# Two message-passing layers on one core: the first edge stage moved to an edge-major tile, half- and quarter-array matrix products, and longer scans in the second edge stage

## The reference

```python
xs = jnp.concatenate([x[edge_src, :8], x[edge_dst, :8]], axis=1)
xv = jnp.concatenate([x[edge_src, 8:].reshape(E, 8, 3), x[edge_dst, 8:].reshape(E, 8, 3)], axis=1)
y1, y2 = _sph(edge_vec)
h = 2.0 ** 0.5 * jax.nn.relu(emb @ W1 / 10.0 ** 0.5)
w = (h @ W2 / 16.0 ** 0.5).reshape(E, 7, MUL, MOUT)
...
s_out = PW_S * (jnp.einsum('eu,euw->ew', xs, wa_s) + INV_SQRT3 * jnp.einsum('eui,ei,euw->ew', xv, y1, wb_s))
...
edge_ftr = jnp.concatenate([s_act, (gates[:, :, None] * v_out).reshape(E, 24)], axis=1) * norm[:, None]
return jax.ops.segment_sum(edge_ftr, edge_dst, num_segments=N)
...
e = s_src[src] + s_dst[dst]
e = jnp.where(e >= 0, e, LEAKY_SLOPE * e)
m = jax.ops.segment_max(e, dst, num_segments=N)
ex = jnp.exp(e - m[dst])
denom = jax.ops.segment_sum(ex, dst, num_segments=N)
alpha = ex / denom[dst]
out = jax.ops.segment_sum(h[src] * alpha[:, None], dst, num_segments=N)
```

## Time and profile before

| | us |
|---|---|
| median of three runs | 6804.19 |
| the profiled execution | 6803.31 |
| its span, first to last instruction | 6801.6 |
| stretch of the 400 groups of the first edge stage (545 to 4075) | 3530 |
| node stage (4090 to 4378) | 288 |
| gathers of the second edge stage (4378 to 6618) | 2240 |
| from its last gather to the next block (6618 to 6647) | 29 |
| last node stage (6647 to 6802) | 155 |

### The profile page before, as it was taken

One profiled execution on the slowest core, in us unless ns is written; L12 is line 12 of the kernel. 1 busy time (PEld: TensorE's weight loads), 2 busy tenths in 40 slices (PEclk: granted clock), 3 DMA queues, 4 the chain that ended last, 5 costly groups with the idle time before them and its releaser, 6 DMA issues. The chain is left out here.

```text
span 6801.6 us, 56405 instructions
## 1 busy us (share of the span) xinstructions
PE 3324.4 (49%) x12859; PEld 1615.4 (24%) x12859; DVE 3604.2 (53%) x5475; ACT 2499.0 (37%) x3555; POOL 4713.2 (69%) x4419
## 2 busy tenths in 40 slices
PE   0008999999999999999999980000000000000000
PEld 0004444444444444444444440000000000000000
DVE  5326887888888888888887872022222221222122
ACT  0006767666666666676766650000000000000000
POOL 4467777777777777777777727776666676677665
PEclk9999999999999999999999995555555555555555
DMA  3511111111111111111111100011111111111111
GB/s 144 179 37 27 31 30 31 29 31 31 27 31 30 31 31 27 29 31 30 31 31 29 22 13 18 10 21 27 27 25 21 29 26 25 24 27 26 25 24 24
DMA packets 266126, 228.09 MB, mean 34 GB/s; under 512 B 181312, under 2 KB 242565, under 8 KB 263406
## 3 DMA queue, kind: packets, MB, share of 16 engines
q0 software_dynamic: 121824, 79.09, 8.1%
q1 hardware_dynamic: 144082, 147.06, 6.7%
HBM read 137.59 MB, written 88.34 MB: 33 GB/s over the span
## 5 line engine op out<-in xcount | busy, mean ns | idle before, releaser
L1159 POOL DMA_INDIRECT gxb<-tab_d,idxb x1600 | 1536.2, 960 | 707.1 <-issue 652.5
L541 POOL DMA_INDIRECT gx<-in_x,idx x1540 | 1670.4, 1085 | 411.3 <-issue 370.9
L868 DVE TENSOR_TENSOR prod<-G_ps,hid 128x1000 f32<-128x1000 f32 x1200 | 1423.1, 1194 | 636.3 <-PE G_ps L744 297.2
L758 PE MATMUL R_ps<-sums,red 128*48 128x500 f32 x2400 | 1290.6, 621 | 0.0
L1251 PE MATMUL R_ps<-dm,ones 125*125 125x125 f32 x2 | 0.8, 494 | 2557.0 <-DVE dm L1280 2557.0
L637 ACT ACTIVATE FT<-T_ps 128x500 fp32r<-128x500 f32 x1200 | 706.9, 589 | 514.1 <-PE T_ps L727 309.1
L727 PE MATMUL T_ps<-ident,HL 125*128 125x125 f32 x4800 | 750.2, 279 | 251.8 <-ACT HL L631 171.8
L548 POOL TENSOR_TENSOR sums<-prod 128x500 f32<-128x500 f32 x400 | 503.0, 1257 | 505.5 <-DVE prod L868 304.0
L1166 ACT ACTIVATE ex<-ex 125x80 f32<-125x80 f32 x40 | 10.8, 269 | 2212.3 <-DVE one_d L1200 1433.6
L1212 DVE TENSOR_TENSOR_SCAN Zb<-dec,Zb,wx 125x40 f32<-125x40 f32 x1280 | 333.6, 294 | 721.1 <-issue 719.7
L727 PEld LDWEIGHTS T_ps<-ident,HL 125*128 125x128 f32 x4800 | 572.3, 143 | 466.1 <-ACT HL L631 172.1
(11 more groups left out here) (195 smaller groups left out, 4152.0 us busy)
## 6 DMA issues: line engine op xcount, KB each, us to landing
y_d<-Zb SPq DMA_DIRECT2D x40, 664.1 KB
gx<-in_x,idx POOLq DMA_INDIRECT x1600
gxb<-tab_d,idxb POOLq DMA_INDIRECT x1600
xd_d<-zeros SPq DMA_DIRECT2D x16, 1562.5 KB
xv<-xd_d SPq DMA_DIRECT2D x40, 625.0 KB
y_d<-zr SPq DMA_DIRECT2D x40, 625.0 KB
em<-in_edge_attr SPq DMA_DIRECT2D x40, 195.3 KB
kp<-keep_d SPq DMA_DIRECT2D x40, 156.2 KB
```

Of the source, the lines that this page charges most:

```text
L541: nc.gpsimd.indirect_dma_start(out=gx[h][:, c * DIM:(c + 1) * DIM], out_offset=None, in_=x, in_offset=bass.IndirectOffsetOnAxis(idx[h][:, ...
L758: last = Tn.matmul(R_ps[0:NOUT, 0:GW], red[:, i * NOUT:(i + 1) * NOUT], sums2[k][:, i * GW:(i + 1) * GW], start=(i == 0), stop=(i == 2))
L868: V.tensor_tensor(prod[i][:, :].rearrange("p (a e) -> p a e", a=2), gv, hid[k][:, :].rearrange("p (a e) -> p a e", a=2), ALU.mult).then_in ...
L1159: nc.gpsimd.indirect_dma_start(out=gx[h][:, c * T1:(c + 1) * T1], out_offset=None, in_=tab_d, in_offset=bass.IndirectOffsetOnAxis(idx[h][: ...
```

## The change

**First edge stage.** F and gx go. One tile `edge` holds 80 columns (a ring of 10 pieces of 8 columns) edge-major, 96 numbers of one edge side by side: 48 of the source end and 48 of the destination end. POOL gathers straight into it, from a copy of x with reordered features that the first block now writes to DRAM (xp_d). POOL does nothing else in the stage; a gather of a piece waits until `low` has read what lay in it. ACT places the scanned destination rows and the edge numbers. `turned` (two DVE products of 192 elements) and `along` (one DVE reduction of 384) take the place of the chunk-wide product and POOL's additions. `high` is two ACT copies of 384 for a piece, `low` two DVE subtractions of 384, and `low_again` goes.

PE transposes two tiles for a group instead of three, into two PSUM buffers, from overlapping 128-column windows of HL. The hidden part is one accumulated pair of matmuls on rows 64 to 127, and one relu; hid is 500 columns and is read twice by `multiply`. Each of the three products is four matmuls that use half of the array's rows: (l, a) = (0,0), (0,1), (1,0), (1,1), where a picks rows 0 to 63 or 64 to 127 and its own PSUM bank, and l the high or low part. The additions on DVE and POOL go. `reduce` is six float32 matmuls, each of which uses 32 of the 128 columns of the array, at i = 0, 1, 2 in turn. `back` reads 96 rows instead of 48. POOL's last step of the message (L561) goes to DVE.

**Second edge stage.** wx and Z are feature-major with a carry column ahead of each feature; three scans of 451 elements replace the 33 of 40. ACT copies the result into a tile of its own, zr, which SP stores.

```diff
-    NT = 3
-    QF = 80
-    FD = QF + NEMB
-    FW = NT * KF
-    HJ = HID // 2
+    SD = 48
+    EW = 2 * SD
+    NT = 2
     SB = 400
     ZEARLY = 12
-    EARLY = 60
+    EARLY = 7
...
+    sp.wait_ge(S("a_xp"), 2)
+    sp.dma_start(xp_d.rearrange("(p k) f -> p (k f)", k=NP), xp[0:P, :]).then_inc(S("a_tab"), 16)
...
+    V.tensor_copy(xpv[:, :, 8:32].rearrange("p k (a u) -> p k a u", a=3), xnv[:, :, 8:32].rearrange("p k (u a) -> p k a u", a=3)).then_inc(S("a_xp"), 1)
+    V.tensor_copy(xpv[:, :, 0:8], xnv[:, :, 0:8]).then_inc(S("a_xp"), 1)
...
+    def gather(s, t):
+        if s % PC == 0:
+            pool.wait_ge(S(f"b_idx{s // PC}"), t * 16 + 16)
+            pool.sem_inc(S("go"), 1)
+        for c in range(s * PW, (s + 1) * PW):
+            nc.gpsimd.indirect_dma_start(out=edge_c[:, c, 8:8 + DIM], out_offset=None, in_=xp_d,
+                                         in_offset=bass.IndirectOffsetOnAxis(idx[c // C][:, c % C:c % C + 1], 0)).then_inc(S(f"b_gx{s}"), 16)
+
+    for s in range(EARLY, RING):
+        gather(s, 0)
+    with pool.Fori(0, PAIRS - 1) as t:
+        for s in range(RING):
+            pool.wait_ge(S("b_lo"), t * RING + s + 1)
+            pool.sem_inc(S("go"), 1)
+            gather(s, t + 1)
...
+    def high(p, s, ch):
+        act.wait_ge(S("b_al"), p + 1)
+        act.wait_ge(S("b_em"), ch * 2 + 2)
+        if later(p):
+            act.wait_ge(S("b_T"), p * 2 * NT - 2 * NT)
+        for d in range(2):
+            A.activation(HLv[s % 2][:, :, :, 0, d], tiles(s)[:, :, :, d], ACT.Copy).then_inc(S("b_hi"), 1)
...
+            col0 = (g % 2 * GT + c) * HW + (64, 0)[i]
+            last = Tn.transpose(T_ps[i][:, c * P:(c + 1) * P], HL[g // 2 % 2][:, col0:col0 + 128].bitcast(f32), ident[0:P, 0:P])
...
+    def hidden(n, k):
+        pe.wait_ge(S("b_FT"), n * NT + 1)
+        for l in range(2):
+            last = Tn.matmul(T_ps[0][:, 0:GW], wh[64:128, l * 128:(l + 1) * 128], FT[k][64:128, 0:GW], start=(l == 0), stop=(l == 1))
...
+            for a in range(2):
+                c0 = 0 if i == 2 and a == 1 else GW
+                last = Tn.matmul(G_ps[(k * 3 + i) % 2][:, a * 512:a * 512 + GW], wst[a * 64:(a + 1) * 64, (2 * i + l) * 128:(2 * i + l + 1) * 128],
+                                 FT[k][a * 64:(a + 1) * 64, c0:c0 + GW], start=(l == 0), stop=(l == 1))
...
+    def reduce(n, k):
+        pe.wait_ge(S("b_mul"), n * 3 + 3)
+        if some(n):
+            pe.wait_ge(S("b_rt"), n)
+        for a in range(2):
+            for i in range(3):
+                last = Tn.matmul(R_ps[32 * i:32 * i + 32, 0:GW], red[:, a * KF:(a + 1) * KF], prod[k][i][:, a * GW:(a + 1) * GW], start=(a == 0), stop=(a == 1))
+        last.then_inc(S("b_R"), 1)
...
+            last = Tn.transpose(Y_ps[0:P, (k * GT + c) * NOUT:(k * GT + c) * NOUT + 96], rt[k][:, c * P:(c + 1) * P],
+                                ident[0:96, 0:96].rearrange("p (i a f) -> p a i f", a=4, f=MO))
...
+    def turned(p, s, ch, h, t):
+        dve.wait_ge(S(f"b_gx{s}"), t * 16 * PW + 16 * PW)
+        dve.wait_ge(S("b_dc"), ch * NPC + NPC)
+        dve.wait_ge(S(f"b_ld{h}"), t * 64 + 64)
+        if some(p):
+            dve.wait_ge(S("b_al"), p)
+        c0 = s % PC * PW
+        nv = dr[h][:, c0 * 3:(c0 + PW) * 3].rearrange("p (c a u) -> p c a u", a=3, u=1).broadcast_to([P, PW, 3, 8])
+        for d in range(2):
+            ev = slot(s)[:, :, d * SD + 16:d * SD + 40].rearrange("p c (a u) -> p c a u", a=3)
+            last = V.tensor_tensor(tmp[:, :].rearrange("p (c d a u) -> p c d a u", d=2, a=3, u=8)[:, :, d], ev, nv, ALU.mult)
+        last.then_inc(S("b_tv"), 1)
...
+        V.tensor_reduce(slot(s).rearrange("p c (d f) -> p (c d) f", d=2)[:, :, 0:8], tv.rearrange("p cd a u -> p cd u a"),
+                        AX.X, ALU.add).then_inc(S("b_al"), 1)
...
+            last = V.tensor_tensor(HLv[s % 2][:, :, :, 1, d], tiles(s)[:, :, :, d], HLv[s % 2][:, :, :, 0, d].bitcast(f32), ALU.subtract)
...
+        V.tensor_tensor(prod[k][i][:, :].rearrange("p (a e) -> p a e", a=2), gv,
+                        hid[k][:, :].rearrange("p (a e) -> p a e", a=1).broadcast_to([128, 2, GW]), ALU.mult).then_inc(S("b_mul"), 1)
...
-        V.tensor_tensor(sums2[k][:, GW:3 * GW].rearrange("p (i e) -> p i e", i=2), q[:, :, 0], q[:, :, 1], ALU.add).then_inc(S("b_add"), 1)
...
+        if i == 2:
+            dve.wait_ge(S("b_yr"), m * 2 + 2)
+            V.tensor_tensor(ov[:, :, 8:32].rearrange("p c (w a) -> p c w a", a=3), pbv,
+                            pgv.rearrange("p c (w a) -> p c w a", a=1).broadcast_to([P, PW, MO, 3]), ALU.mult).then_inc(S("b_o"), 1)
...
+            FS = T1 // 3
+            dec = sbt("dec", [P, FS * C1])
...
-        sp.wait_ge(S(f"d_z{h}"), t + 1)
-        sp.wait_ge(S(f"d_zm{h}"), t + 1)
-        sp.dma_start(y1_d[0:E, :].rearrange("(p c) f -> p (c f)", c=EP)[:, bass.ds(ch * C * R1, C * R1)], Z[h][:, :]).then_inc(S(f"d_st{h}"), 16)
+        sp.wait_ge(S(f"d_zr{h}"), t * 2 + 2)
+        sp.dma_start(y1_d[0:E, :].rearrange("(p c) f -> p (c f)", c=EP)[:, bass.ds(ch * C * R1, C * R1)], zr[h][:, :]).then_inc(S(f"d_st{h}"), 16)
...
+        nc.scalar.activation(wx[:, DIM * C1 + 1:T1 * C1], ex[:, 0:C], ACT.Exp).then_inc(S("d_exp"), 1)
+        nc.scalar.activation(ex[:, C:2 * C], ex[:, C:2 * C], ACT.Exp).then_inc(S("d_exp"), 1)
+        act.wait_ge(S(f"d_st{h}"), t * 16)
+        act.sem_inc(S("go"), 1)
+        zo = zr[h][:, :].rearrange("p (c f) -> p c f", f=R1)
+        nc.scalar.activation(zo[:, :, DIM + 1], mx[h][:, 1:C1], ACT.Copy).then_inc(S(f"d_zr{h}"), 1)
+        act.wait_ge(S(f"d_z{h}"), t + 1)
+        nc.scalar.activation(zo[:, :, 0:T1], Zv[h][:, 1:], ACT.Copy).then_inc(S(f"d_zr{h}"), 1)
...
-        V.tensor_tensor_scan(out=zv[:, :, DIM], data0=dec[:, :], data1=ex[:, 0:C], initial=zp[:, C - 1, DIM:DIM + 1],
-                             op0=ALU.mult, op1=ALU.add)
-        for f in range(DIM):
-            last = V.tensor_tensor_scan(out=zv[:, :, f], data0=dec[:, :],
-                                        data1=wx[:, :].rearrange("p (c f) -> p c f", f=DIM)[:, :, f],
-                                        initial=zp[:, C - 1, f:f + 1], op0=ALU.mult, op1=ALU.add)
+        dve.wait_ge(S(f"d_zr{h}"), t * 2)
+        dve.sem_inc(S("go"), 1)
+        for i in range(3):
+            part = slice(i * FS * C1, (i + 1) * FS * C1)
+            last = V.tensor_tensor_scan(out=Z[h][:, part], data0=dec[:, :], data1=wx[:, part], initial=0.0, op0=ALU.mult, op1=ALU.add)
...```

PE, the middle of a turn in the first edge stage, before (G_ps are the products, H_ps the hidden numbers, T_ps the transposes, R_ps the sums, Y_ps the transposes back):

```order
L748 MATMUL G_ps0<-FT0,wst 128x500
L758 MATMUL R_ps<-sums1,red 48x500
L734 MATMUL H_ps<-FT1,wh 128x500
L727 MATMUL T_ps<-ident,HL1 128x125 x4
L758 MATMUL R_ps<-sums1,red 48x500
L744 MATMUL G_ps1<-FT1,wst 128x500 x2
L727 MATMUL T_ps<-ident,HL1 128x125 x4
L758 MATMUL R_ps<-sums1,red 48x500
L744 MATMUL G_ps0<-FT1,wst 128x500 x2
L768 MATMUL Y_ps<-ident,rt0 125x48 x4
L734 MATMUL H_ps<-FT0,wh 128x500
```

More of the change, by code:

```diff
@@ L529, in _ @@
                     turn(PAIRS - 1, last=True)
[L530 to L531 removed]
+                    store(NCH - 1)
                     sp.wait_ge(S("b_st"), 16 * NCH)
@@ L564, in turn @@
-                    def turn(t, first=False, last=False):
-                        for g in range(G2):
-                            add(t * G2 + g, g % 2)
-                            if g % GC == 5 and not (last and g > GC):
-                                along(t * 2 + g // GC + 1, 1 - g // GC)
-                            if not last:
-                                gather(g % GC * GT, GT, g // GC, t + 1)
-                            if g % 2 == 0 and not (first and g < 4):
-                                pq = (g - 4) // 2 % GC
-                                gates(t * GC + (g - 4) // 2, pq // (GC // 2), pq % (GC // 2))
@@ new lines, in turn @@
+                            if not last and gc in (6, 7):
+                                spread(2 * gc - 12, ch + 2, h, t + 1)
+                                spread(2 * gc - 11, ch + 2, h, t + 1)
+                            if not (first and h == 0) and gc in (5, 8):
+                                i = 0 if gc == 5 else 2
+                                gather_sums(i, ch - 1, 1 - h, t - 1 + h)
+                                gather_sums(i + 1, ch - 1, 1 - h, t - 1 + h)
+                            if not (last and g >= G2 - 2):
+                                for i in range(NT):
+                                    out_of_T(n + 2, k, i)
+                                relu(n + 2, k)
@@ L703, in _ @@
                             out_of_T(n, n, i)
-                    for i in range(2):
-                        relu(0, 0, i)
+                        relu(n, n)
                     turn(0, first=True)
@@ L794, in turn @@
                             if more2:
[L795 to L797 removed]
+                                transposes(n + 2, g2, p2, 0)
```

(9 more changed lines are left out.)

688 lines of the change are left out of this document (279 added, 409 removed).

## The result

The changed kernel takes 7420.9 us (median of four runs, 7414.8 to 7428.5), the kernel before beside it 6813.8 (6795.2 to 6824.2): a ratio of 1.0897, 95% interval 1.088 to 1.0913. It is slower by 9%, where 6030 us were forecast.

The account below looks back on a forecast made before the run. PE was taken as the bound, with its own work for 8.0 of 8.83 us a group in the first edge stage. 6803.3 - 572 (first edge stage) - 210 (second) + 10 (start) = 6031, rounded 6030; eight-in-ten range 5680 to 6600 us.

Parts of the forecast that it names:

- The rate of PE's own work: First edge stage: PE's transposes, back, hidden, products and six sums add up to 7.24 us a group.
- in steps: First edge stage, six sums on PE: only neighbouring passes of successive strips overlap, seven steps of 0.42 plus change-over, 3.1 us.
- rival 1: First edge stage: the sums overlap better, lower end 1.94 us, group about 6.5, total 5670 us; chance 0.11.
- the Trainium skill's figure for three strips: First edge stage, PE: three column strips run 2.38 times as fast, six sums 2.45 us, time about 5790.
- The waiting on top, 0.16 us a group: First edge stage: PE's waits add 0.16 us to its own work, making 7.4 us a group, a gain of 572 us.
- below PE: First edge stage: POOL only gathers, 54 us a chunk of ten groups, a load still below PE's.
- Rival 4: Slow issue, 1.40 us apart on DVE, comes into the first edge stage: 7200 us or more; chance 0.03.
- So I cost these waits at nothing: First edge stage: POOL's waits for `low` and for indices, loaded 12 groups ahead of their first use, cost 0.
- The second edge stage, 210 us: Second edge stage: three long scans bring POOL's indices in time, so its pauses go, saving 210 of 224 us.
- The carry copy and a wider wx lie inside this: Second edge stage: these extras fit in the index chain, some 44 us after lk where POOL needs indices at 51.
- The start, 10 us: Start: early gathers wait for x to be loaded, reordered and written out, costing 10 us, bounds 0 and 30.

Follow-up runs that it names:

- k2: The changed kernel with one of every eight gathers kept in the first edge stage's loop, timed where the kernel before takes 6803 to 6814 us: 5665 us.
- k1: The changed kernel itself, nothing altered, timed again where the kernel before takes 6803 to 6814 us: 7388 us, ratio 1.086.
- d3: The changed kernel, but POOL loads a chunk's indices itself once the gathers two chunks back have landed, in rows of 8 gathers: 6767 us, ratio 0.995.
- m1: The changed kernel itself, nothing altered, timed where the kernel before takes 6565 to 6570 us: 5536 us, ratio 0.843.
- d5: The kernel before with only the second edge stage's change (three scans of 451, ACT copies, SP waits): 6783 us, ratio 0.997.
- h1: The changed kernel with POOL's own index loads and a 0.25 us pause after every fourth gather, where the kernel before takes 6565 to 6570: 5534 us, ratio 0.8433.
- k3: The changed kernel with POOL's own index loads and a 0.25 us pause after every fourth gather, where the kernel before takes 6803 to 6814: 6000 us, ratio 0.8815.

## Why the prediction was wrong, point by point

**The rate of PE's own work: right mechanism, a term too large.** The group on PE was put at 7.24 us and takes 5.77. Products with row halves overlap (0.65 for 0.66), the transposes take 0.57 and 0.48, back 0.5, hidden with the product behind it 1.1. Six changes between whole, halved and quartered array in a group cost nothing that these intervals show. The six sums were put at 3.1 "in steps" and take 1.81: the three strips run wholly side by side, which was rival 1, and its lower end 1.94 was the measurement within 0.13. The step that failed here was the argument that the second pass of one sum blocks the next strip. The estimate from the Trainium skill's figure for three strips (2.45 us, by "TensorE: Matmul & The Clock Gate", Part 3) was too high as well. DVE came to 2256 / 400 = 5.6 us a group for 5.86, ACT to 3.6 for "under 4.9".

**The waiting on top, 0.16 us a group: the step that turned the sign.** A group takes 10.49 us where PE's own work is 5.77, so the waits are 4.7 us. They are results of PE that reach ACT and DVE late, by 6 to 37 us, in one group of ten: 43 us a chunk (k2 against k1), 1723 in all. The forecast had looked at POOL's 54 us a chunk only as a load ("below PE") and never asked what a row of 40 gathers does to the others.

Rival 4, at 0.03, came nearest. It had the condition ("seen only where POOL issues nothing but gathers, and now POOL does that in both"), and that was met. Its mechanism, DVE's instructions 1.40 us apart, isn't what costs the time in the trace: the two products of DVE shown above stand 32 us apart, behind waits of 7.33 and 31.08 us for a semaphore. That its 7200 or more agrees with 7421 is therefore in part luck. The two are akin at least, for the trace of before has the lateness itself, on DVE, around the pause of the earlier trace rows:

```profile
4521.58 0.30 DVE L1212 TENSOR_TENSOR_SCAN Zb<-dec,Zb,wx 125x40 f32<-125x40 f32 x1 [1.10 <-issue]
4531.94 0.18 DVE L1189 TENSOR_SCALAR rst<-kpb 125x40 f32<-125x40 f32 x1 [10.06 <-remote]
```

The last scan ends at 4521.88, and both DVE, which waits for it at L1189, and SP, whose store starts at 4531.58, learn of it 10 us later. The prediction read the pause as the store waiting for scans; without the late signal the store could have started 10 us sooner. In the chunks whose scans begin 2 us after such a pause, all 32 of them stand 0.2 us apart; in those that begin 9 us after it, six do and then the spacing of 0.7 to 1.4 sets in. Still, the row of gathers isn't the whole condition: in the second edge stage of the changed kernel gathers follow one another as closely, and DVE's steps from lk to the last scan take 7.9 us, as on a quick occasion (8.0 in m1). What else it takes stays open.

**"So I cost these waits at nothing": right.** The 2130 us of waiting for indices look like the cause and aren't one: d3 removes them and the stage still takes 8.85 us a group; on a quick occasion m1 keeps the old chain and loses nothing.

**The second edge stage, 210 us: wrong.** The pauses went, as forecast, and POOL is the bound, but I had it gather at its old pace. By the groups 190 us of POOL's idle time went (707 to 517), and 164 came back as longer gathers (1536 to 1700); the time fell by 20 (d5). "The carry copy and a wider wx lie inside this" was true of the index chain and false of POOL. The kernel before takes 238 us less on a quick occasion, about the 224 of its pauses; no trace of it was taken there, so that the pauses are the difference is inferred, and so is that the long scans gain nothing there.

**The start, 10 us:** the first product of DVE starts at 533.0 instead of 534.5, so nothing.

**The sum again, with measured terms.** On quick occasions: 6566 - 5536 = 1030 us, more than the 772 of the forecast and less than the 1133 of rival 1. On a slow-issue one: 6803 - 1084 for the first stage as k2 has it ((8.81 - 6.10) x 400) - 20 for the second = 5699, against 5665 measured for k2. The rows of gathers, 1723 us, are the whole of the 1390 by which the forecast was too low, and more.

## What to carry to other kernels

When a change leaves an engine with nothing but gathers to issue, break their row up: a pause of 0.7 us after every fourth, with index loads that don't lag, was worth 1500 us here on the occasions that need it, and cost 140 on those that don't. A pause of 0.25 us (h1, k3) cost nothing on a quick one and was worth 1388 on a slow-issue one (7388 to 6000), so here it is the safer choice where the kind isn't known. An engine far from its own bound can still set the time by what it does to the others' semaphores, so a condition seen in one stage ("only where POOL issues nothing but gathers") has to be asked of every stage that comes to meet it. And before a kernel is judged, it is worth running it on more than one occasion: this one is 9% slower or 16% faster.
